# Last layer of a two-layer gated cross-attention block: both centre products of a pair of channel tiles on ScalarE

## The reference, cut to what matters

```python
def act_quant(x):
    scale = 127.0 / jnp.clip(jnp.max(jnp.abs(x), axis=-1, keepdims=True), 1e-05)
    return jnp.clip(jnp.round(x * scale), -128, 127) / scale
...
h = bit_linear(x, w1)                      # 512 -> 2048, ternary weights, int8 activations
h = depthwise_conv1d(h.transpose(0, 2, 1), conv_w, conv_b)   # three taps along the tokens
h = h.transpose(0, 2, 1)
h = jax.nn.silu(h)
return bit_linear(h, w2)                   # 2048 -> 512
...
x = x + jnp.tanh(g_ffn[1]) * _L1_ffn_ref(_layernorm(x, axis=-1), ...)
```

## Time and profile before

| | |
|---|---|
| median of 3 runs | 1818.0 us (1815.43 to 1829.16) |
| the profiled execution, its own time | 1819.27 us |
| its span, first to last instruction | 1817.5 us |
| mean granted TensorE clock | 0.938 of full speed |
| busy: TensorE / VectorE / ScalarE / GpSimd | 1568.5 / 1273.3 / 887.4 / 578.0 us |

### The profile page before, as it was taken

One profiled execution on the slowest core, in us unless ns is written; L12 is line 12 of the kernel. 1 busy time (PEld: TensorE's weight loads), 2 busy tenths in 40 slices (PEclk: granted clock), 3 DMA queues, 4 the chain that ended last, 5 costly groups with the idle time before them and its releaser, 6 DMA issues. The chain is left out here.

```text
span 1817.5 us, 25655 instructions
## 1 busy us (share of the span) xinstructions
PE 1568.5 (86%) x9526; PEld 955.6 (53%) x9559; DVE 1273.3 (70%) x2058; ACT 887.4 (49%) x1434; POOL 578.0 (32%) x557
## 2 busy tenths in 40 slices
PE   4788889888768979978999999999997878888886
PEld 3444444443346638755666665666664534444443
DVE  3367778778643555655677776777756699999995
ACT  3355555454444526525343333433432477777763
POOL 3124342232420002113112121111200397777770
PEclk9899999999887889989999999999998899999999
DMA  4112112212442343541011202102011321211111
GB/s 158 47 47 93 57 60 70 93 70 70 167 180 82 115 176 104 197 145 47 1 59 35 71 25 59 59 24 82 1 58 36 131 109 52 74 67 64 53 47 47
DMA packets 73235, 142.34 MB, mean 78 GB/s; under 512 B 8369, under 2 KB 17733, under 8 KB 72858
## 3 DMA queue, kind: packets, MB, share of 16 engines
q1 hardware_dynamic: 72154, 137.55, 21.8%
q0 software_dynamic: 960, 3.15, 0.6%
HBM read 97.67 MB, written 43.01 MB: 77 GB/s over the span
## 5 line engine op out<-in xcount | busy, mean ns | idle before, releaser
L2800 POOL TENSOR_TENSOR E_y<-E_y,E_centre 128x1024 f32<-128x1024 f32 x64 | 151.2, 2363 | 10.1 <-ACT E_y L2829 7.8
L1395 ACT ACTIVATE D_oT<-D_OB 128x512 fp32r<-128x512 f32 x64 | 38.3, 599 | 223.0 <-DVE D_OB L1712 223.0
L2715 PE MATMUL E_OP<-E_w2q,E_yb 128*128 128x512 bf16 x509 | 125.6, 403 | 25.0 <-issue 18.9
L2792 POOL TENSOR_SCALAR E_centre<-E_hs,E_cw,E_cb 128x512 f32<-128x512 f32 x64 | 108.6, 1697 | 57.7 <-DVE E_hs L2882 57.4
L2705 PE MATMUL E_HP<-E_xT,E_w1q 128*128 128x512 bf16 x482 | 121.2, 391 | 2.3 <-ACT E_xT L2806 0.4
L1684 DVE TENSOR_TENSOR D_q_low<-D_PJ,D_q_high 128x512 fp32r<-128x512 f32 x60 | 41.5, 691 | 94.9 <-ACT D_q_high L1371 94.9
L2891 DVE SCALAR_TENSOR_TENSOR E_y<-E_hs,E_cw,E_y 128x512 f32<-128x512 f32 x128 | 107.1, 875 | 0.0
L1464 PE MATMUL D_PJ<-D_xT_high,D_wq_high 128*128 128x512 f32 x240 | 100.6, 419 | 0.1
L2715 PEld LDWEIGHTS E_OP<-E_w2q,E_yb 128*128 128x128 bf16 x512 | 51.6, 103 | 92.6 <-issue 44.0
L573 PE MATMUL A_TX<-A_wo,A_oT 128*128 128x512 f32 x176 | 90.6, 640 | 7.1 <-PEq L1048 7.1
L1464 PE MATMUL D_PJ<-D_xT_high,D_wq_low 128*128 128x512 f32 x240 | 94.3, 393 | 0.0
(11 more groups left out here) (403 smaller groups left out, 4153.3 us busy)
## 6 DMA issues: line engine op xcount, KB each, us to landing
A_x<-in_x SPq DMA_DIRECT2D x8, 1024.0 KB, 5.4
A_res<-in_x SPq DMA_DIRECT2D x8, 1024.0 KB, 5.5
xn_d<-A_xn SPq DMA_DIRECT2D x8, 1024.0 KB, 4.7
x_d<-A_res SPq DMA_DIRECT2D x8, 1024.0 KB, 6.2
W_raw<-in_w1T SPq DMA_DIRECT2D x16, 512.0 KB, 3.7
W_raw<-in_w2T SPq DMA_DIRECT2D x16, 512.0 KB, 3.7
D_res<-x_d SPq DMA_DIRECT2D x8, 1024.0 KB, 6.0
x_d<-D_res SPq DMA_DIRECT2D x8, 1024.0 KB, 4.5
```

The lines of the kernel that those rows point to most:

```text
L2715: mm = pe.matmul(OP[:, :], yb[:, k, c * P:(c + 1) * P], w2q[:, k, :], start=k == 0, stop=k == MC - 1)
L2792: pool.tensor_scalar(U[i % 2][:, 0, :], hs[i % NBUF][:, 0, 1:TILE + 1], cw[:, 2 * p, 1:2], cb[:, 2 * p:2 * p + 1], ALU.mult, ALU.add).then ...
L2800: pool.tensor_tensor(y, y, U[i % 2][:, :, :], ALU.add).then_inc(t0, 1)
```

## The change

ScalarE takes over the centre product of the even channel tile, with its bias, right behind that of the odd tile and ahead of both left products. GpSimd keeps the halo columns and the sum; its waits for the scaled pair and for the free centre buffer go with the product. Nothing else changes: same buffers, same semaphores, same functions of the other engines.

```diff
@@ gpsimd queue
                 for p in range(MP):
                     i = MP * n + p
-                    pool.wait_ge(h_s, i + 1)
-                    need(pool, t0, i - 1)
-                    pool.tensor_scalar(U[i % 2][:, 0, :], hs[i % NBUF][:, 0, 1:TILE + 1], cw[:, 2 * p, 1:2],
-                                       cb[:, 2 * p:2 * p + 1], ALU.mult, ALU.add).then_inc(ce, 1)
                     if i + 1 < MP * STEPS:
                         halo((i + 1) // MP, (i + 1) % MP)
                     pool.wait_ge(tl, 2 * (i + 1))
@@ scalar queue, products(n, p)
                 need(act, t0, i - 1)
                 act.activation(U[i % 2][:, 1, :], hs[i % NBUF][:, 1, 1:TILE + 1], ACT.Copy,
                                scale=cw[:, 2 * p + 1, 1:2]).then_inc(co, 1)
+                act.activation(U[i % 2][:, 0, :], hs[i % NBUF][:, 0, 1:TILE + 1], ACT.Identity,
+                               bias=cb[:, 2 * p:2 * p + 1], scale=cw[:, 2 * p, 1:2]).then_inc(ce, 1)
                 act.wait_ge(h_halo, i + 1)
```

## The result

The changed kernel takes 1842.9 us (median of 4 runs, 1837.8 to 1845.6) against 1819.4 us (4 runs, 1815.4 to 1829.2) before: a ratio of 1.0121, 95% interval 1.0096 to 1.0146. It is slower, by 23.5 us. The forecast was 1834 us with a range of 1815 to 1843: the sign is right and the size is two thirds of what came, at the very edge of the range.

A forecast was written before the change was run, and what follows sets the result against it. VectorE was taken to bound a steady step, GpSimd only the first stretch. Casts 4.9, held pairs 9.1, first step 1.0 and tail 0.5 sum to +15.5, rounded to 16 us on 1818.0: 1834 us, range 1815 to 1843.

The forecast's parts named there:

- The held pair of p3: VectorE's tap pair in a step's fourth pair: waits for GpSimd's sum under the port lock, +1.61 us a step.
- In p4 the pair: VectorE's tap pair in a step's fifth pair: loses 0.10 us surplus, net +1.51 us in six steps, +9.1 us.
- The cast's 0.70 us: ScalarE's tile-0 cast behind the sixth pair's products: 0.70 us later, uncovered, seven times, +4.9 us.
- The clock: Rival, TensorE behind its gap: another slow output product on the path each step, 10 us more, 1844 us; chance 0.08.
- The pair of p2: VectorE's tap pair in a step's third pair: gets the lock first, takes 1.41 us, sum follows; gain 0.
- The first step: Step without casts, bound by GpSimd: freed but lock remains, 4.36 us a pair against 4.23, +1.0 us.
- The tail: End of the layer: the last sum, 0.70 us later, reaches into the last-but-one tap pair, +0.5 us.
- GpSimd's relief worth nothing in a steady step: Steady step: GpSimd losing its centre products takes nothing directly from the path, as its sum waits for ScalarE's left products.
- Faster, 1801 us: Rival, decided in a step's third pair: earlier GpSimd sums remove the right taps' surplus, 17 us less; chance 0.12.
- No second collision, 1823 us: Rival, a step's fourth pair: sum starts later or tap pair goes first, only the casts' 4.9 us remain; chance 0.15.

The follow-up runs named there:

- Experiment 8: The changed kernel with all four casts of a step moved ahead of the products of their pair on ScalarE: 1817.5 us.
- Experiment 2: The changed kernel with only the cast of token tile 0 moved ahead of the products of its pair on ScalarE: 1821.6 us.
- Experiments 5 and 6: The kernel before (5) and the changed kernel (6), each with twelve extra matmuls in TensorE's gap ahead of the tile-0 output product: 1811.0 and 1825.0 us.
- experiment 4: The changed kernel with GpSimd also making its old centre product, into a spare buffer nobody reads: 1842.4 us.
- experiments 1, 7: The kernel before with the tile-0 cast alone (1) or all four casts (7) moved ahead of their pair's products: 1810.2 and 1808.9 us.
- experiment 3: The kernel before with the even tile's centre product made on no engine, its buffer half zeroed once: 1813.0 us.

## Why the prediction was right or wrong, point by point

**The sum, by one step.** Counted from the quantising of tile 3 (1641.49 before, 1651.38 after):

| up to | before | after | added | predicted |
|---|---|---|---|---|
| end of the tap pair of p3 | 20.13 | 21.75 | +1.62 | +1.61 |
| end of the tap pair of p4 | 24.54 | 26.08 | +1.54 | +1.51 |
| the tile-0 addition | 39.87 | 43.31 | +3.44 | +2.21 |
| a step | 44.35 | 47.78 | +3.43 | +2.21 |

*The held pair of p3* is right in place and in what it adds, and wrong in its form. The sum of p2 starts 18.18 us after the quantising, 18.16 were predicted, and the pair ends 1.21 us after the sum's end, as the row before had it (1.22). The range had this collision between 1.2 and 1.9 us; no row gives the upper bound, and +1.62 was measured. But the pair was to take about 3.0 us, and takes 2.17: it starts 0.86 us later, because p2 is longer. Experiment 8 shrinks the hold by moving the sum, and shows it to be the cause. In p4 the pair was to lose its surplus of 0.10 us. It grew to 1.64 us instead, and what made up for it was 0.2 us less on a small instruction of the token units between the pairs (0.17 us and not 0.37); that the net came out as +1.54 against +1.51 is luck.

*The cast's 0.70 us* is right: from the first product of p5 to the cast 3.08 us before, 3.78 after (1682.62 to 1686.40). Experiment 2 takes it away.

*The clock* is the term that failed. The prediction left the output product at 5.07 us, put another slow product in each step down as a rival with a chance of 0.08 and a price of 10 us, and took nothing of it into the sum. The product became 6.26 us: 1.19 us a step, which closes the table (1.54 + 0.70 + 1.19 = 3.43). In six steps it was not a second product that fell to the low level but the same one, for twice as long; in the first step it was a product that had run at full clock (3.61 us, then 6.16). By rows that is 9.8 us, and with the forecast's +15.5 it makes 25.3 of the layer's 26.4. Experiments 5 and 6 put it, with a part of the cast, at 10.3 us. I had seen that the gap grows from 3.15 to 3.9 us, and had argued that the product could as well gain; experiment 4 shows it may, in every other steady step of one execution, while in the changed kernel's profiled execution it did in none.

*The pair of p2* is wrong in its form and right in its effect. It was to take 1.41 us with the sum behind it. It takes 3.52: the sum came 0.48 us after the first tap had begun, 0.46 were predicted, but it got in between the two taps and held the second. The step that failed is to have taken the two taps for one holder of the lock. The reduction comes 17.32 us after the quantising, and came at 16.45. That 0.87 us is not in the total, for the pair of p3 is released by the sum of p2 in either case.

*The first step*: from the first scale to the ninth 35.6 us before, 36.7 after, +1.1 against the predicted 1.0. Counted from the scale of p4 to that of the next p4 it is 34.9 and 35.6, +0.7, and the kernel before with the casts moved (experiments 1, 7) had 34.9 and 35.9 there, so the size is not told from the difference between executions. *The tail*, from the last quantising of tile 3 but one to the end, is +0.4, predicted 0.5; between experiments 1 and 2 it is +1.8, so this agreement may be luck.

*GpSimd's relief worth nothing in a steady step* is right (experiment 3), with 2.4 us in the first step, which the changed kernel does not have: its first step is 1.1 us longer.

**The rivals.** Faster, 1801 us: out, with experiment 3 at 1813 us even without the price. No second collision, 1823 us: out by the row at 1670.96. The clock, 1844 us: this is the rival that came, with 9.8 us by rows against the 10 that it was priced at, though over the same product and not over another. Its chance of 0.08 rested on no row; that the product could escape was argued, while six of the seven in the kernel before were slow already.

## What to carry to other kernels

Here moving work off an engine that did not bound the loop gained nothing in a steady step, and what it cost on the other engine was not the busy time (5.6 us a step) but each chain that stood behind it in that queue (3.4 us a step). Walk one period of the loop with the durations of the rows: here the ends of two held pairs came out within 0.03 us, though the form of each hold did not. Where a chain ends at TensorE behind a gap, price the gap's clock too: here 0.7 us more of a gap came with 1.2 us more of product in six steps of seven, and 2.5 us more in the first. And look for work that stands behind a wait it doesn't need: moving the casts ahead of the products gave 7 to 8 us (experiments 1 and 7), where relieving GpSimd at no price to ScalarE gave 5 (experiment 3).

## What the runs showed of the hardware that was not expected

- Between two back-to-back VectorE instructions with two SBUF operands each, GpSimd can get in. The sum that asked 0.48 us after the first tap's start ran next (2.49 us), and the pair took 3.52 us. The centre product of the kernel before, asking 0.2 to 0.3 us after the first tap's start, waited for both taps (1.70 to 1.78 us, 0.77 alone). What decides between them was not tested.
- Halving the GpSimd instruction shortened one hold and not the other. The pair of p3, which came behind the sum, ends where it did (3.52 against 3.57 us after the sum's start), for the engines take turns. The pair of p2, which the sum had cut in two, fell from 3.52 to 2.42 us.
- A gap of 3.85 us in TensorE's work was followed by an output product of 3.61 us in one step and of 5.30 us in another of the same execution, and in the changed kernel of 6.21 to 6.26 us in step after step. A gap of 3.15 us was followed by 5.0 us in most steps and by 3.61 in one (experiment 3). What decides how long the low level lasts was not tested.
